# Queries of an image's last three tiles projected behind the key-value sums, and group averages over interleaved channels

## The reference

```python
def layer0(x, Wq, bq, Wk, bk, Wv, bv, Wfc, bfc):      # x is a group norm of the input, 32 groups of 12 channels
    q = apply_rope_2d(conv1x1(x, Wq, bq))
    k = apply_rope_2d(conv1x1(x, Wk, bk))
    v = conv1x1(x, Wv, bv)
    q = elu(to_heads(q) * scale) + 1.0                # 6 heads of 64
    k = elu(to_heads(k)) + 1.0
    v = to_heads(v)
    kv = einsum('bhnd,bhne->bhde', k, v)              # sum over all 4096 tokens of the image
    k_sum = k.sum(axis=2)
    normalizer = einsum('bhnd,bhd->bhn', q, k_sum)[..., None]
    out = einsum('bhnd,bhde->bhne', q, kv) / (normalizer + 1e-06)
    return conv1x1(merge_heads(out), Wfc, bfc)
def layer1(x, fft_filter, w_in, w_dw, w_out):         # x is a group norm again
    t = einsum('bchw,oc->bohw', x, w_in)
    t = irfft2(rfft2(patches_8x8(t)) * fft_filter)
    t = depthwise_conv_3x3(t, w_dw)
    return einsum('bchw,oc->bohw', gelu(t[:, :192]) * t[:, 192:], w_out)
x = x + layer0(_gn(x), ...)
x = x + layer1(_gn(x), ...)
```

## Time and profile before

| | us |
|---|---|
| median of 3 runs | 3549.17 (3548.68 to 3550.89) |
| profiled execution | 3545.66 |
| its span, first to last instruction | 3543.9 |
| PE busy in it | 3318.6 (94%) |
| DVE busy | 2981.3 (84%) |
| ACT, POOL busy | 1723.4, 2042.9 |
| mean granted TensorE clock | 0.981 of full |

### The profile page before, as it was taken

One profiled execution on the slowest core, in us unless ns is written; L12 is line 12 of the kernel. 1 busy time (PEld: TensorE's weight loads), 2 busy tenths in 40 slices (PEclk: granted clock), 3 DMA queues, 4 the chain that ended last, 5 costly groups with the idle time before them and its releaser, 6 DMA issues. The chain is left out here.

```text
span 3543.9 us, 50201 instructions
## 1 busy us (share of the span) xinstructions
PE 3318.6 (94%) x17374; PEld 2872.3 (81%) x17374; DVE 2981.3 (84%) x5231; ACT 1723.4 (49%) x3159; POOL 2042.9 (58%) x1343
## 2 busy tenths in 40 slices
PE   5999999999999999999999999998999999999998
PEld 4987779877797778977789777896779967799775
DVE  7877989779898798887989879888798887888887
ACT  2433854338443474435744257442664426644275
POOL 2555755547556475564755647456565565655665
PEclk9999999999999999999999999999999999999999
DMA  6215332143321432123332233213332133331422
GB/s 224 72 36 178 106 109 72 54 161 107 122 67 63 143 132 100 63 85 125 130 101 70 90 133 124 100 54 111 113 125 99 54 131 113 113 101 52 143 99 98
DMA packets 185341, 369.89 MB, mean 104 GB/s; under 512 B 7771, under 2 KB 8835, under 8 KB 184835
## 3 DMA queue, kind: packets, MB, share of 16 engines
q1 hardware_dynamic: 185090, 366.68, 30.3%
HBM read 265.99 MB, written 100.66 MB: 103 GB/s over the span
## 5 line engine op out<-in xcount | busy, mean ns | idle before, releaser
L1136 PE MATMUL bank<-w_hi,x_hi 128*128 128x384 f32 x2304 | 803.5, 349 | 17.9 <-ACT vt L578 10.7
L444 POOL TENSOR_TENSOR t<-t 128x768 f32<-128x768 f32 x256 | 535.3, 2091 | 466.4 <-DVE t L841 462.4
L1137 PE MATMUL bank<-w_lo,x_hi 128*128 128x384 f32 x2304 | 781.7, 339 | 0.0
L1007 DVE SCALAR_TENSOR_TENSOR bank<-big,wdw,bank 128x512 f32<-128x512 f32 x1072 | 749.1, 746 | 20.4 <-PE bank L1317 17.3
L437 POOL TENSOR_TENSOR x_lo<-xa,x_hi 128x512 fp32r<-128x512 f32 x360 | 459.4, 1292 | 478.4 <-ACT x_hi L567 478.4
L509 POOL TENSOR_TENSOR prod<-prod 128x512 f32<-128x512 f32 x320 | 410.5, 1283 | 244.5 <-ACT prod L670 224.9
L1141 PE MATMUL bank<-w_hi,x_lo 128*128 128x384 f32 x2304 | 533.1, 339 | 0.5 <-POOL x_lo L437 0.5
L572 ACT ACTIVATE t<-t 128x384 f32<-128x384 f32 x256 | 134.7, 526 | 759.5 <-POOL t L444 747.8
L1136 PEld LDWEIGHTS bank<-w_hi,x_hi 128*128 128x128 f32 x2304 | 436.8, 190 | 23.9 <-issue 22.7
L1137 PEld LDWEIGHTS bank<-w_lo,x_hi 128*128 128x128 f32 x2304 | 437.3, 190 | 1.1
L1141 PEld LDWEIGHTS bank<-w_hi,x_lo 128*128 128x128 f32 x2304 | 415.0, 189 | 1.4 <-POOL x_lo L437 1.4
(11 more groups left out here) (132 smaller groups left out, 6966.8 us busy)
## 6 DMA issues: line engine op xcount, KB each, us to landing
xr<-x SPq DMA_DIRECT2D x128, 768.0 KB, 4.7
xa<-x SPq DMA_DIRECT2D x64, 768.0 KB, 6.3
x_scratch<-xr SPq DMA_DIRECT2D x64, 768.0 KB, 3.3
xa<-x_scratch SPq DMA_DIRECT2D x64, 768.0 KB, 6.0
xr<-x_scratch SPq DMA_DIRECT2D x64, 768.0 KB, 4.8
out<-xr SPq DMA_DIRECT2D x64, 768.0 KB, 3.3
big<-x SPq DMA_DIRECT2D x8, 768.0 KB, 10.2
w_raw<-wqkv_t SPq DMA_DIRECT2D x1, 1728.0 KB, 6.8
```

The lines of the kernel that those rows point to most:

```text
L444: nc.gpsimd.tensor_tensor(a, a, b[:, :, ::-1, :], ALU.add).then_inc(s_add, 1)
L1007: nc.vector.scalar_tensor_tensor(dst, src, wdw[:, k, q:q + 1], so_far, ALU.mult, ALU.add)\
L1136: nc.tensor.matmul(dst, hi(k), whi(k), start=(k == 0), stop=False)
L1137: nc.tensor.matmul(dst, hi(k), wlo(k), start=False, stop=False)
```

## The change

Two independent edits and one small one.

1. **Late queries.** The tiles 29, 30 and 31 of an image (`NLATE = 3`, all in the last chunk) project only keys (one block of nine, both halves through a strided view of the weights) and values in stage A. Their queries are projected by `late_project`, one block of nine each, into banks 4, 5 and 7: that of tile 29 behind the sums of tile 29, that of tile 30 behind the sums of tile 31, and that of tile 31 behind the transposition of the key-value sums. The fillers of 6, 4 and 2 are gone, those of 10 become 8. Bias, rotation, elu of these queries (`late_bias`, `late_rope` on DVE, `late_sum` on POOL, `late_exp` on ACT, `late_elu` on DVE) stand between the steps of the transition and of the first chunk of B. For the keys of these tiles the DVE, POOL and ACT steps are half as wide. DVE's query product (944 before) reads the key sums from PSUM (bank 0) instead of `kbc`. `mout_lo`, `qt_hi` and others get other places in memory, so that the x parts of the last chunk live longer; u1 and u2, scratch for the late queries, lie over the second half of `xa`.
2. **Channels as c = 3p + k.** x, the output, x1 and the input weights are viewed as (p k) instead of (k p): a partition holds three neighbouring channels, and a group of 12 is four partitions. `group_avg` makes three products instead of seven in each round, and mean, variance, scale and shift have one column instead of three. The rows of weights and biases are permuted on the host to match. A chunk's transfer still moves 128 x 3 rows of 2 KB each; neighbouring partitions are now 48 KB apart in DRAM instead of 16 KB.
3. **Last chunk of B.** The output block 0 of the last chunk goes through ACT and POOL (`proj`) instead of DVE, and DVE takes block 1 first, then the statistics of 0 and 1, then block 2 and its statistics.

```diff
+NLATE = 3
-GBLOCKS = [(k, m) for m in range(KB) for k in range(KB) if abs(k - m) <= 1]
-    x_v = x.rearrange("b (k p) (c n) -> b p k c n", p=P, n=CHUNK)
+    x_v = x.rearrange("b (p k) (c n) -> b p k c n", p=P, n=CHUNK)
...
+        QBANK = (4, 5, 7)
...
+                late_sum(0)
                 gp.wait_ge(s_ka, i * 5 + 1)
...
                                         kbc[:, :].unsqueeze(1).to_broadcast([P, TG, C]), ALU.mult).then_inc(s_prod, 1)
+                late_sum(1)
...
                         times_ksum(c + 1, 1 - par)
+                    if c == 0:
+                        late_sum(2)
...
+                gp.wait_ge(s_xr[1], (i * 12 + 8) * 16)
+                gp.wait_ge(s_proj, i * NCH + NCH)
+                nc.gpsimd.tensor_tensor(xr[:, 1, 0], xr[:, 1, 0], proj[:, :], ALU.add).then_inc(s_sum, 1)
...
+            def late_bias(i, u):
+
+                dve.wait_ge(s_lproj, i * NLATE + u + 1)
+                q = bank[QBANK[u]][:, 0:C].rearrange("p (b f) -> p b f", b=2)
+                nc.vector.tensor_tensor(q, q, by_part(qkbias[:, :], 0), ALU.add).then_inc(s_lbias, 1)
+
+            def late_rope(i, u, halves=(0, 1)):
+
+                dve.wait_ge(s_lbias, i * NLATE + u + 1)
+                dve.wait_ge(s_lelu, max(i * NLATE + u - 1, 0))
+                tile = NT - NLATE + u
+                tabs = [(t_cosh[:, tile, :], t_sinh[:, tile, :]), (t_csw[:, 0, :], t_csw[:, 1, :])]
+                for b in halves:
+                    for dst, tab in zip((u1, u2), tabs[b]):
...
+                        else:
+                            dve.wait_ge(s_lo, (i * 16 + NCH) * 3 + 6)
+                            late_bias(i, 0)
+                            late_rope(i, 0, (0,))
                         elu(T + j, c * 4 + j, j % 2)
                 steps(NCH, part_a)
+                late_rope(i, 0, (1,))
...
+                late_rope(i, 1)
                 dve.wait_ge(s_kd, i * 5 + 5)
                 denominators(0, 0)
                 divide_q(0, 0)
+                late_bias(i, 2)
+                late_rope(i, 2)
...
+                    if c == 0:
+                        late_elu(i, 1)
+                        late_elu(i, 2)
...
-                    for m in range(KB):
-                        ks = [k for k, mm in GBLOCKS if mm == m]
-                        for k in ks:
-                            ins = nc.tensor.matmul(bank[7][:, 2 * m:2 * m + 2], t_gavg[:, GBLOCKS.index((k, m)), :], src(k),
-                                                   start=(k == ks[0]), stop=(k == ks[-1]))
+                    for k in range(KB):
+                        ins = nc.tensor.matmul(bank[7][:, 0:2], t_gavg[:, :], src(k), start=(k == 0), stop=(k == KB - 1))
...
+            def late_project(u, par):
+
+                tok = slice((TPC - NLATE + u) * P, (TPC - NLATE + u + 1) * P)
+                split_product(bank[QBANK[u]][:, 0:C], lambda k: x_hi[:, par, k, tok], lambda k: x_lo[:, par, k, tok],
+                              lambda k: by_part(w_hi[:, k, 0:2 * C], 0), lambda k: by_part(w_lo[:, k, 0:2 * C], 0))\
+                    .then_inc(s_lproj, 1)
...
+                    if edge == NCH - 1:
+                        late_project(0, par)
                     add_kv(T + 2, 2)
...
-                    if edge == NCH - 1:
-                        keep_warm(6, 0)
                     add_kv(T + 3, 3, last=(edge == NCH - 1))
...
-                keep_warm(4, 5)
+                late_project(1, 1)
...
-                keep_warm(2, 5)
                 pe.wait_ge(s_kd, i * 5 + 4)
                 for j in range(KB):
                     ins = nc.tensor.transpose(bank[1][:, j * P:(j + 1) * P], kvfix[:, j], ident)
                 ins.then_inc(s_kp, 1)
+                late_project(2, 1)
...
-                keep_warm(10, 5)
-                transpose_q(0, 0)
+                pe.wait_ge(s_lrope, i * NLATE + 2)
+                keep_warm(8, 5)
+                transpose_q(0, 0, frees=True)
```

199 lines of the change are left out of this document (136 added, 63 removed).

## The result

| | us |
|---|---|
| before, median of 4 runs | 3550.03 (3548.68 to 3552.57) |
| after, median of 4 runs | 3515.17 (3514.0 to 3515.7) |
| ratio after to before | 0.9901, 95% interval 0.9883 to 0.9918 |
| profiled span after (before: 3543.9) | 3513.2 |
| forecast | 3479, range 3463 to 3504 |

The changed kernel is faster by 35 us, half of the 70 that were forecast, and outside the range. The direction was right, the size was not. The two profiled spans differ by 30.7 us.

A forecast was written before the change was run, and what follows sets the result against it. PE, busy 94%, was taken to set the time, waiting at the A-to-B transition and the group norm. Gains of 49.6 + 16.6 + 3.0 + 0.8 = 70 us took 3549.2 to 3479 us, range 3463 to 3504.

The forecast's parts named there:

- Late queries up to the transposition: Transition A to B, tile 29 to first transposition: gain 6.2 us per image, between 5.1 at low clock and 7.2.
- (b): Late sum 1 on POOL, about 1.1 us, stays hidden between product and division, where POOL waited 2.57 us.
- (c): Late queries of tile 31 on PE delay output-weight products about 1.0 us; the wait at the next fillers covers it.
- (d): Tile 31's bias and four halves, 1.7 us on DVE behind the division, where DVE waited 1.39 us: 0.3 us shows.
- Cover (a): Before the denominators: DVE's added late work ends at 21.6, just before POOL's product at 21.66; used up to the last tenth.
- the rule of the shared ports: GpSimd is slowed by Vector instructions with two SBUF inputs; POOL's query product would end 0.35 us sooner, 0.1 us an image at most.
- Cover (e): First chunk of B: late sum 2, last two elus and exponentials fit where POOL and DVE wait (2.5 us), costing nothing.
- Layout: Transfers with the same 2 KB rows at other distances: price taken as 0, as no row shows it.
- My rival for it: Distances of 48 KB slow all transfers: 3589 us at twice the time, deciding from about 65% slower; chance 0.03.
- Group average: Group norm, B to C: cheaper rounds gain 2.1 us per image, 16.6 in all; chunk 0's transfer is late next, at 6.0.
- lost to the transfer: Rival: new distances make chunk 0's transfer 1 us or more later, 3487 and up to 3496 us; chance 0.08.
- Start: Program's start: both group-average rounds gain with no transfer waiting, 1.9 to 3.5 us, taken as 3.0.

## Why the prediction was wrong, step by step

- **Late queries up to the transposition: right, the term under-sized.** Schedule 26.39, measured 26.37, with errors of 0.1 to 0.4 us on the way that cancel. Covers (b) and (c) held. Of (d), 0.2 us shows in the second image (second part of the first transposition 2.28 us behind the first instead of 2.10, forecast 0.3). I took 6.2 as the middle between full and half clock; the clock was full in all images, 7.2. PE idles 1.18 us ahead of the sums of 31 (2.01 before), and the late block of tile 30 stands behind them as work; that this kept the clock up was not tested.
- **Cover (a)** was a tenth of a microsecond, and it did not hold as written: DVE's late rotation ends 0.47 us behind POOL's product, which came first. It cost nothing against the schedule, because POOL was earlier and DVE was free when it had been forecast to be. That DVE was free then hangs on its operand in PSUM: with the sums in SBUF it is 1.3 us an image more. There I had let the rule of the shared ports act on POOL alone, and had not asked who starts first; this gap in the reasoning had no part in the missed time, since the changed kernel reads PSUM.
- **Cover (e)**, "late sum 2, the last two elus and their exponentials stand in the first chunk of B, where POOL and DVE wait again; cost nothing": this step failed. I counted instructions at their undisturbed length against a wait. Both of their operands lie in SBUF, and POOL's running division and product hold them up: 5.0 us instead of 1.1, of which 1.6 to 1.7 reach PE. 14 us in all, shown by the exponentials in PSUM (3501.2 us).
- **Layout, "No row shows its price ... I take 0":** this step failed, and cost most. A store takes 0.45 us more from the start of the issue to the landing, 0.2 of it the issue; loads of a chunk take 0.3 to 0.4 more. It counts at three places of an image where SP's transfers are on the path: 0.9 at B's end, 1.1 in the load of chunk 0 with another 0.94 behind it through the clock, and 1.25 at A's start. Layout alone: 0.23% slower than before, where 20 us faster was forecast; without the layout the late queries reach 3502.1 us. My rival for it blamed the distance and asked for 65% longer transfers before it decided; the distance is not the cause, and medians 6 to 14% longer sufficed to eat the layout's own gain. The edit also shifted what lies behind the smaller arrays in SBUF; the prediction has no step for that.
- **Group average, 2.1 us:** its own part was right. The averages are ready 5.7 us behind the aggregation; the transfer is late next, as said. But it landed in 7.0, not 5.8, so 0.85 was left. That was the rival "lost to the transfer" (1 us or more later), which I gave 0.08, though with another cause than the distances; with the transfer mended the stretch takes 5.57.
- **Last chunk of B, 0.1:** 0.0. With the old layout third transposition to aggregation is 54.5 us in both kernels.
- **Start, 3.0:** 3.9. Aggregation to normalisation gave 3.5 of it (11.13 to 7.65 us), the upper bound: DVE waits 1.61 us for each round instead of 3.32. The rest is an earlier input, and part of it is lost again before tile 29.
- **The 2.6 in C and A** are thus 0.94 at C's start, 1.25 at A's start and 0.41 of drift, the places in SBUF. Of the 0.8 that the late queries show without the layout, 0.3 lies at A's start and 0.4 just ahead of it; that was not taken further.

The range failed with the two zeros. Both were named as steps, and neither got an upper bound in the range. Either of them mended alone brings the time into it.

## What to carry over

A new view of a tensor can make its transfers dearer even if rows, bytes and count stay. Where an image has several transfers on its path, a tenth of a transfer decides, so run a changed view alone before an edit is built on it. When work is moved beside a running POOL instruction, look at where its operands lie, not only at its length: a VectorE instruction with two operands in SBUF waits for the whole POOL instruction if it comes second, and one operand in PSUM avoids that. And when small arrays shrink, see whether the main loop still has its period and the stores still land as before.

## What I had not expected of the hardware

- An elementwise VectorE instruction of 384 columns with both operands in SBUF took 3.85 us beside a POOL product of 3.80, 0.55 with one operand in PSUM; in the pairs that start almost together, the second waits: POOL 2.48 instead of 1.84, or VectorE 2.27 instead of 0.94.
- A transfer of 128 x 3 rows of 2 KB at one uniform DRAM stride: issue 0.54 to 0.58 us, store landing in 3.8. The same rows with each partition's three in falling order: 0.37 and 3.5, the whole difference before the first packet. In one piece of 768 KB: 0.32 and 3.3.
- 72 bytes a partition less in small arrays: 0.016 us more per tile in a loop of 5.42 us, and 0.12 us more until a store of 2 KB rows lands.
